# The opening of a fused layer-norm and linear-attention kernel, rebuilt

## The reference, cut to what matters

```python
def ffn(x):                       # s_len = 2, n_head = 16: cap = s_len // n_head = 0
    y = x                         # no token is routed
    return (y - mean(y)) * rsqrt(var(y) + 1e-5) * ln_g + ln_b
def attn(x):                      # 16 heads of 32, causal linear attention
    q, k, v = x @ Wq.T, x @ Wk.T, x @ Wv.T
    pq, pk = elu(q) + 1, elu(k) + 1
    S, z = cumsum(pk[:, None] * v[None, :]), cumsum(pk)
    return (pq @ S) / (pq . z + 1e-5) @ Wo.T + bo
x = x + 0.5 * ffn(layernorm(x))
x = x + attn(layernorm(x))
x = x + 0.5 * ffn(layernorm(x))
```

## Time and profile before

| | |
|---|---|
| median of 3 runs | 927.04 us (925.59 to 927.11) |
| the profiled execution | 928.43 us, its span 926.7 us |
| PE busy | 895.8 us, 97% of the span |
| DVE, ACT, POOL busy | 832.2, 753.7, 705.0 us |
| chain that ended last | PE 87%, DMA 4%, DVE 3%, issue 3% |
| granted TensorE clock | 0.995 over the span |

### The profile page before, as it was taken

How to read it: one execution, slowest core, us unless ns; L and a number is a source line. 1 busy time by engine, 2 the same in 40 slices (tenths; PEclk the granted TensorE clock), 3 DMA queues, 4 the chain that set the end, 5 groups by cost and what they waited for, 6 DMA issues and landing times.

```text
span 926.7 us, 29932 instructions
## 1 busy us (share of the span) xinstructions
PE 895.8 (97%) x10252; PEld 525.3 (57%) x10252; DVE 832.2 (90%) x1537; ACT 753.7 (81%) x1301; POOL 705.0 (76%) x869
## 2 busy tenths in 40 slices
PE   3999999999999999999999999999999999999995
PEld 2555555555556656555655555665555565555562
DVE  7889889899999999999999999999999999989787
ACT  5888788888888888888888888888888888888682
POOL 3268777788777789777778877778977778987672
PEclk9999999999999999999999999999999999999998
DMA  7576798766687666677767678767668776767783
GB/s 249 131 146 134 150 180 157 131 150 150 145 181 158 140 146 148 147 166 158 159 137 153 146 152 174 160 137 151 148 145 172 158 153 141 143 132 138 131 138 98
DMA packets 421564, 139.80 MB, mean 151 GB/s; under 512 B 402576, under 2 KB 402832, under 8 KB 421520
## 3 DMA queue, kind: packets, MB, share of 16 engines
q1 hardware_dynamic: 404496, 106.73, 61.2%
q10 hardware_dynamic: 17024, 32.51, 10.5%
HBM read 21.76 MB, written 16.78 MB: 42 GB/s over the span
## 4 chain that ended last, share of the span: by engine, by line
PE 87%; DMA 4%; DVE 3%; issue 3%; ACT 1%; POOL 1%; SPq 0%; DVEq 0%; ACTq 0%; POOLq 0%
PE PJ L1596 49%; PE PJ L1701 16%; PE AV L1675 8%; PE SC L1648 6%; PE AV L1687 5%; PE AV L1672 3%; DMA AT<-ATTN 2%; DMA KS<-KN 1%; DMA X<-in_L_attn_x_dram 1%; DMA shift<-in_L_ffn_ln_b_dram 1%; DVE AM L1166 1%; PE SC L1573 0%; DVE TP L1290 0%; POOL A L500 0%; POOL X1BO L433 0%
## 5 line engine op out<-in xcount | busy, mean ns | idle before, releaser
L1596 PE MATMUL PJ<-wT,XT 128*128 128x512 f16 x2304 | 526.0, 380 | 0.2
L1596 PEld LDWEIGHTS PJ<-wT,XT 128*128 128x128 f16 x2304 | 217.7, 98 | 245.1 <-issue 4.7
L500 POOL TENSOR_TENSOR A<-AM,A 128x512 f16<-128x512 f32 x252 | 288.0, 1162 | 30.4 <-ACT A L783 30.4
L1701 PE MATMUL PJ<-wT,AT 128*128 128x512 f16 x768 | 176.0, 379 | 1.2 <-DMA AT<-ATTN 1.2
L490 POOL TENSOR_SCALAR_AFFINE_SELECT AM<-AM 128x512 f32<-128x512 f32 x124 | 78.9, 636 | 114.4 <-ACT AM L770 114.4
L783 ACT ACTIVATE A<-AM 128x512 f16<-128x512 f32 x256 | 153.7, 631 | 12.0 <-POOL AM L490 9.9
L1675 PE MATMUL AV<-VN,A 128*128 128x33 f16 x3072 | 116.4, 177 | 0.0
L1701 PEld LDWEIGHTS PJ<-wT,AT 128*128 128x128 f16 x768 | 71.1, 97 | 78.8 <-DMA AT<-ATTN 2.7
L1672 PE MATMUL AV<-SS,QS 128*128 128x33 f16 x1024 | 111.7, 178 | 0.0
L1675 PEld LDWEIGHTS AV<-VN,A 128*128 128x128 f16 x3072 | 108.8, 96 | 3.7
L1166 DVE TENSOR_TENSOR AM<-SC,causal 128x512 f32<-128x512 f32 x132 | 89.8, 683 | 19.9 <-PE SC L1648 19.7
(11 more groups left out here) (113 smaller groups left out, 1520.4 us busy)
## 6 DMA issues: line engine op xcount, KB each, us to landing
out_dram<-Y ACTq DMA_DIRECT2D x31, 512.0 KB, 3.2
X<-in_L_attn_x_dram ACTq DMA_DIRECT2D x30, 512.0 KB, 3.5
X<-in_L_attn_x_dram SPq DMA_DIRECT2D x2, 512.0 KB, 7.9
A<-in_L_attn_Wk_dram SPq DMA_DIRECT2D x1, 1024.0 KB, 9.0
A<-in_L_attn_Wq_dram SPq DMA_DIRECT2D x1, 1024.0 KB, 11.2
QS<-in_L_attn_Wv_dram SPq DMA_DIRECT2D x1, 1024.0 KB, 15.5
XT<-XH SPq DMA_TRANSPOSE x64, 3.4
QS<-in_L_attn_Wo_dram SPq DMA_DIRECT2D x1, 1024.0 KB, 5.7
```

The costliest lines, as they stand in the source:

```text
L500: g.tensor_tensor(A[:, b, LO, hg], AM[:, k % 4], A[:, b, HI, hg], ALU.subtract).then_inc(a_lo.sem, 1)
L1596: ins = t_.matmul(PJ[b], XT[:, w, c, b * C:(b + 1) * C], wT[m_][:, m, c, :], start=(c, w, m) == todo[0], stop=(c, w, m) == todo[-1])
L1701: ins = t_.matmul(PJ[b], AT[:, b, w, c * C:(c + 1) * C], wT[3][:, m, c, :], start=(c, w, m) == todo[0], stop=(c, w, m) == todo[-1])
```

## The change: the opening in a new order and with other means

The loop and the closing keep their lists. In the opening:

- Chunk 0 is loaded by tiles (`load_x_tile`), with W_K between the two and W_Q behind them; W_O is loaded right behind W_V and no longer behind the first transposing transfers.
- Gain, shift and bias come as single rows of 2 KB, issued by ACT. PE spreads each over the partitions by a float32 matmul with a column of halves or ones (`spread_row`), and ACT copies it out of PSUM (`keep_row`). DVE's two halvings go.
- The statistics' roots of chunk 0 are made by tiles (`rstd0_of_tile`, `rstd1_of_tile`). DVE normalises chunk 0 (`normalise_first`), PE turns it (`turn_first`, into the banks `TP`), and ACT and DVE write the halves straight to `XT` (`x_half_first`, `x_low_first`); the two transposing transfers go.
- The projections of chunk 0 wait for a quarter of their weight before each third matmul, not for the whole.
- W_O's quarters go through `AV2[:, 1]` and `AV2[:, 0]` alone; `scores` of chunk 0 no longer wait for them, the first `attend` does.
- POOL clears `S` and `SS`, and DVE's five small memsets wait for each other no more.
- All five lists of the opening have a new order.

```diff
-        W_BANKS = PJ + [spare[k % 3] for k in range(4 * GROUPS - 2)]
+        W_BANKS = PJ + [spare[k % 3] for k in range(3 * GROUPS - 2)] + [AV2[:, 1], AV2[:, 0]] * 2
...
+            def load_x_tile(b):
+                sp.dma_start(X[:, 0, b], x[b, 0:C, :]).then_inc(x_loaded[0] if b else x_first, 16)
...
-                load_bias()
-                early.turn_x(0)
-                early.turn_x(1)
+                load_x_tile(0)
+                load_w(0)
+                load_x_tile(1)
+                load_w(1)
+                load_x(1)
+                load_w(2)
                 load_w(3)
...
+            g.memset(S[:], 0.0).then_inc(state_zeroed, 1)
+            g.memset(SS[:], 0.0).then_inc(state_zeroed, 1)
...
+            for i, (row, loaded) in enumerate(((ln_g, gain_loaded), (ln_b, shift_loaded), (attn_bo, obias_loaded))):
+                a.dma_start(rows[i], row.rearrange("(a n) -> a n", a=1)).then_inc(loaded, 16)
...
+            def keep_row(i):
+                act.wait_ge(row_spread, i + 1)
+                a.activation((gain, shift, obias)[i][:], spare[i][:], ACT.Copy).then_inc(rows_kept, 1)
...
+                    def x_half_first(b):
+                        act.wait_ge(x_first_turned, b + 1)
+                        a.activation(XT[:, HI, :, b * C:(b + 1) * C], TP[b][:].rearrange("p (c t) -> p c t", t=C),
+                                     ACT.Copy, scale=X_UP).then_inc(x_hi.sem, 1)
...
+                    def normalise_first(b):
+                        dve.wait_ge(*stat1_done.upto(f, b))
+                        dve.wait_ge(rstd1_done.sem if b else rstd1_first, 1)
+                        v.tensor_scalar(XN[:, b], X1[:, b], stat1[:, b, 0:1], rstd1[:, b:b + 1], ALU.subtract, ALU.mult).then_inc(xn_done.sem, 1)
...
+                    def x_low_first(b):
+                        dve.wait_ge(*x_hi.upto(f, b))
+                        at = XT[:, :, :, b * C:(b + 1) * C]
+                        v.scalar_tensor_tensor(at[:, LO], TP[b][:].rearrange("p (c t) -> p c t", t=C), X_UP, at[:, HI],
+                                               ALU.mult, ALU.subtract).then_inc(x_lo.sem, 1)
...
+            def spread_row(i):
+                pe.wait_ge((gain_loaded, shift_loaded, obias_loaded)[i], 16)
+                t_.matmul(spare[i][:], (half_row, half_row, ones_row)[i][:], rows[i], start=True, stop=True).then_inc(row_spread, 1)
...
-                if k >= W_REUSE:
+                if 2 <= k < W_REUSE:
+                    pe.wait_ge(rows_kept, k - 1)
+                elif j == 3 and c == 1:
+                    pe.wait_ge(w_scaled, 4)
+                elif j == 3:
+                    pe.wait_ge(wT_lo, k - 1)
+                elif k >= W_REUSE:
...
+            def turn_first(b):
+
+                pe.wait_ge(*xn_done.upto(0, b))
+                for c in range(GROUPS):
+                    ins = t_.transpose(TP[b][:, c * C:(c + 1) * C], XN[:, b, c * P:(c + 1) * P], ident[:])
+                ins.then_inc(x_first_turned, 1)
...
-                def project(m_, b, filled):
+                def project(m_, b, filled, first=False):
                     todo = [(c, w, m) for c in range(GROUPS) for w, m in PASSES]
                     for c, w, m in todo:
+                        if first and (w, m) == PASSES[0]:
+                            pe.wait_ge(wT_lo, W_ORDER.index(m_) * GROUPS + c + 1)
...
             def opening():
                 first, second = ops(Step(0, -1)), ops(Step(0, 0))
+                spread_row(0)
+                spread_row(1)
                 w_turn(0, 0)
+                spread_row(2)
```

More of the change, by code:

```diff
@@ L1397, in opening @@
                 w_low(0, 3)
-                scale_w(1)
-                early.x_low(1)
-                first.front_gain(0)
-                second.front_stats(1)
-                row_sums(2)
+                early.x_low_first(0)
+                early.x_low_first(1)
+                scale_rest(1)
+                top_norm(2)
                 w_low(1, 0)
@@ L1418, in opening @@
                 first.low_k(0)
+                w_low(2, 0)
                 first.front_stats1(0)
+                top_norm(3)
+                first.front_mean1(0)
+                first.phi_k(1)
+                first.phi_q(0)
+                w_low(2, 1)
+                scale_w(3)
                 first.front_stats1(1)
-                row_sums(3)
-                first.front_mean1(0)
+                first.low_q(0)
+                w_low(2, 2)
                 first.front_mean1(1)
-                first.phi_q(0)
+                w_low(2, 3)
@@ L1425, in opening @@
+                second.front_stats(0)
                 first.phi_q(1)
-                top_norm(3)
-                second.front_mean(0)
-                w_low(2, 3)
-                first.low_q(0)
-                scale_w(3)
-                first.low_q(1)
-                w_low(3, 0)
-                first.x_low(0)
+                w_low(3, 0)
+                w_low(3, 1)
+                second.front_stats(1)
+                first.low_q(1)
+                first.x_low(0)
+                first.low_k(1)
```

273 lines of the change are left out of this document (144 added, 129 removed).

## The result

Measured side by side, the kernel before takes 927.08 us (median of 4, 925.59 to 928.01) and the changed one 935.83 us (median of 4, 934.5 to 936.35): a ratio of 1.0097, 95% interval 1.0082 to 1.0112. It is slower by 8.75 us, where 2.1 us of gain were forecast. The profiled execution took 934.5 us, its span 932.8. Each further kernel was measured beside the kernel before on its own chip (medians of the latter there 925.3 to 926.4); ratios are the common measure, and 0.001 of ratio is 0.93 us.

The account below looks back on a forecast made before the run. PE was taken to run without pause from 49.04 us, the opening's end set by ACT and DVE. The walk's 2.0 us gain, rounded to 2.1, gave 926.3 profiled, 924.9 median; 8-in-10 range 922.3 to 927.2.

Parts of the forecast that it names:

- Step 1: Loads in the opening: W_K lands at 7.1 and W_Q at 11.2 us, 4.2 and 2.8 earlier; first row at 3.1.
- Step 2: Scale of W_K in the opening: ready at 13.0 us instead of 15.44, a gain of 2.4, with PE near its slow level.
- Rival A: Opening: PE is fast by the first turns and the whole lead arrives; gain 4.4 us, 922.6; chance 0.24.
- Step 3: First projection of chunk 0: starts at 22.2 instead of 23.31, takes 3.9, ends at 26.1 against 27.7; gain 1.6 us.
- Step 4: From first projection to loop: engine lists walked in order put the mark at 47.0 instead of 49.04, gain 2.0 us.
- the mark: Start of chunk 1's projections on PE, 49.04 us before; the change was held worth what it moves this.
- from there PE doesn't pause: Reading of the earlier profile: from 49.04 us, where chunk 1's projections begin, PE works without pause.
- C: Rival, slower: behind the opening, POOL's `x1_bias` delays `split_a`, wanted by the second `attend`; 928 to 929 us; chance 0.08.
- B: Rival: ACT and DVE eat the lead before the mark; gain 0.95 or less, 926.1 to 926.7 us; chance 0.18.

Follow-up runs that it names:

- e4: Changed kernel with POOL's `x1_bias` moved behind `rstd0_of_x`; ratio 1.0072 to the kernel before.
- e1: Changed kernel with ACT's load of x for chunk 3 (`first.next_x`) back behind the first exponential of q; ratio 1.0057 to the kernel before.
- e2: Changed kernel with DVE's `second.low_k(0)` back ahead of `phi_k(1)`; ratio 1.0075 to the kernel before.
- e3: Changed kernel with the load of x early (e1) and `low_k(0)` early (e2) together; ratio 1.0043 to the kernel before.
- e5: e3 with the semaphore counters starting where they did in the kernel before; ratio 1.0040 to the kernel before.
- e6: Changed kernel with the moves of e1, e2 and e4 and the former counters; ratio 1.0043 to the kernel before.
- a5: e6 with 95 waits added on PE in small portions, its loop 128 instructions further than in the kernel before; ratio 1.0018 to that kernel.
- a2: Changed kernel with 31 more PE instructions ahead of `turn_norm(1)`, its loop 64 further than in the kernel before; ratio 1.0055 to that kernel.
- b4: Kernel before with 16 further instructions on PE ahead of its first turn; ratio 1.0035.
- b7: Kernel before with 32 further instructions on PE ahead of its first turn; ratio 1.0040.
- b3: Kernel before with 67 further waits, packed into 33 instructions, on PE ahead of its first turn; ratio 1.0045.
- a3: e3 with 31 more PE instructions, its loop 64 further than in the kernel before; ratio 1.0023 to that kernel.
- b5: Kernel before with 64 further instructions on PE ahead of its first turn; ratio 0.9996.
- b1: Kernel before with ACT's load of x for chunk 3 moved late, beside the second transposing transfer of x; ratio 1.0012.
- e7: e6 with 31 more PE instructions ahead of `turn_norm(1)`, its loop 64 further than in the kernel before; ratio 1.0022 to that kernel.
- a4: e6 with 31 more instructions at PE's very start, its loop 64 further than in the kernel before; ratio 1.0047 to that kernel.

## Why the prediction was wrong

**Step 1** held. W_K landed at 6.88 (7.1), the first rows of L1611 begin at 2.67 (3.1) and take 3.78 for two (3.8); the square of W_Q began at 10.31, ahead of the 11.2. The first row of 2 KB, issued at 0.80, was there by 2.67, so within 1.9 us, less than the 2.1 that the text took for the least.

**Step 2** held: `w_scale` 13.05 + 0.15 against 13.0, at PE's lower level, as its turns of 1.12 for four show. Rival A is out by this.

**Step 3** failed by one term. The second `normalise_first` was priced at 0.43, "as the halving"; it took 1.86 under POOL's `x1_bias` (the earlier trace rows have that operation before, where no such DVE instruction ran beside it). First projection at 23.93, forecast 22.2. e4 gives back 1.5 us of the 1.7. Its length, 3.81, was forecast as 3.9.

**Step 4**, to the mark: forecast 47.0, measured 48.16, 1.2 us late, about what step 3 was late by (1.7). The exponential of q began at 34.29, not 32.6. The walk was sound, and the gain at the mark 0.9 instead of 2.0.

**The step that failed** is the one ahead of all of them: "from there PE doesn't pause", hence "a shift at its entry arrives whole at the end" and "the loop neither gains nor loses". Each of the three was read from the trace of before and holds for its order only.

- PE pauses behind 49.04 when what it needs there is released later in relation to it. The text never costed `first.next_x`, an issue that the new list puts 13 us later, against `turn_x(1)`, and never asked how far ahead of their reader the transfers behind the mark land. In the kernel before, the second transfer was issued at 47.5 and landed at 50.7, 1.1 us ahead of its reader (49.04 + 2.75); with the new order this margin is gone, and it cost 2.25 us of stop and 1.7 us of the lower clock (e1: 3.7 us).
- `second.low_k(0)` changed places behind the mark with no word about it in the prediction, and with it SP's queue (e2: 2.0 us). The text also holds W_O's quarters hidden, because `attend` needs them only near 55; their last `w_low` on DVE now stand ahead of a `mask` for which PE waits 0.65 to 0.8 us in e3, e5, e6 and a5.
- The same list of instructions ran longer in the loop (2.2 us by the profiles of the changed kernel and a2, 0.0035 to 0.0045 by the medians of b4, b7 and b3), because 33 instructions more stand ahead of it. Nothing in the profile of before could have given this price; but that the loop's speed depends on what is ahead of it was excluded, and should have been a rival.

The sum: 1.0097 less 0.0054 (e3) and 0.0040 (b7; 0.0035 to 0.0045) is 1.0003. (With a2's 0.0042 the 1.7 us of the slow level would be taken off twice.) Taken out together (a3) they leave 1.0023, with the stop that the padding itself brings: from mark to entry a3 takes 2.9 us (0.0031) longer than e3, the stop of 2.3 and slower matmuls behind it. a5 has no such stop and is at 1.0018 all the same. So these causes account for the loss but for some 0.002, for which there are the 1.3 to 1.6 us that e3 and a5 still lose between mark and entry, and what a5's trace doesn't hold. Whether a lead at the mark reaches the end can't be told from the ratios: e6 has its entry 2.1 us earlier than e3, and the same ratio.

**The rivals.** C, the only slow one, named `x1_bias` before `split_a` as the mechanism, behind the second `cut`; the waits of PE from 44 to 80 us are for XT (2.3), AT (1.4) and one of 0.4 on DVE, none on POOL, whose four `split_a` ended at 57.8, ahead of the first `attend` (60.50). B's sign, a mark beyond 48, came (48.16), but its worst time was 926.7. The range's lower end, "A's 922.3", should have read 922.6 by A's own sum. C, with its 928 to 929, ended on the right side for the wrong reason, and with 0.08 for "slower" and an upper end of 927.2 the range had no room for what the new order does behind the mark.

## What to carry to other kernels

A change to a lead-in is worth what it moves only if each transfer behind the mark still lands ahead of its reader: for each, write down its release, its length and its reader before and after, and list every DMA, on any queue, that the new order puts beside it. Before blaming a list of instructions for a slower loop, pad the code ahead of it: if the turn's length changes with the padding, as in b3 (0.2 us at the back edge), it is the code's place. And a stop on the matmul engine can cost more than its own length, since the lower clock may follow (0.75 granted over 6.88 us): 2.25 us made 3.9 in the changed kernel, and only 2.25 in a2.

## What the runs showed of the hardware

- The matmul engine's loop of 1330 instructions (690 operations) loses 0.1 (+16) to 0.2 us at each back edge when its start is moved by 16, 32 or 33 instructions, and nothing when it is moved by 64 or 128: 770 against 772 to 774 us of loop, ratios of 1.0035 to 1.0045 (b4, b7, b3) against 0.9996 (b5).
- A plain load of 512 KB beside a transposing transfer stretches the latter from 3.2 to 5.3 us in the changed kernel (4.9 in b1, 3.3 without the load in e1).
- Behind a packet of 16 KB of instructions in the midst of transposing transfers hardly anything moves for 1.3 to 1.5 us (e7, a3, a4, b5, a2); the one at 44.5 in a5, ahead of the data of a transposing transfer, and the one at 55.75 in e6, behind them, held nothing up.
- A stop of PE of 2.2 to 2.3 us in a busy stretch was followed by matmuls at the lower level in the changed kernel, e2 and e4 (24 in 7.04, 7.04 and 6.93 us, granted clock 0.75 to 0.77), and by none in a2 (5.35 us, 1.00).
- A float32 `tensor_scalar` of 128 x 512 from SBUF on DVE takes 0.50 us alone and 1.86 beside a `tensor_tensor` of POOL of 128 x 1024 (the two `normalise_first` of the changed kernel; the second takes 0.54 in e4, ahead of POOL's).
